# Two edge chunks to a PSUM bank: TensorE up to 12 chunks ahead of VectorE, one semaphore step a pair

## What is computed

```python
h = jnp.maximum(_layernorm(x, axis=-1), 0.0)
hx = jnp.einsum('ni,rio->rno', h, weight)          # 8 relations
msg = hx[edge_type, src]
agg = jax.ops.segment_sum(msg, dst, num_segments=num_nodes)
out = x + agg * 0.5 ** 0.5 + h_bias + (h @ loop_weight) * 0.5 ** 0.5
```

## Time and profile before

| what | value |
|---|---|
| median of the runs | 2552.59 us |
| lowest and highest run | 2542.56 and 2552.97 us |
| span of the profiled execution | 2587.3 us |
| busy: PE, POOL, DVE, ACT | 1645.8, 1552.6, 1297.6, 345.3 us |
| chunks, gathers by GpSimd, tiles | 1661, 1542, 98 |

### The profile page before, as it was taken

How to read it: one execution, slowest core, us unless ns; L and a number is a source line. 1 busy time by engine, 2 the same in 40 slices (tenths; PEclk the granted TensorE clock), 3 DMA queues, 4 the chain that set the end, 5 groups by cost and what they waited for, 6 DMA issues and landing times.

```text
span 2587.3 us, 36344 instructions
## 1 busy us (share of the span) xinstructions
PE 1645.8 (64%) x10568; PEld 1254.5 (48%) x10568; DVE 1297.6 (50%) x4142; ACT 345.3 (13%) x427; POOL 1552.6 (60%) x1646
## 2 busy tenths in 40 slices
PE   0002657766776777777777577667667777767767
PEld 0001445555554555555555455555455555545556
DVE  3273454455454555555455455455544554545444
ACT  2163010110111011011011011111111110111110
POOL 7704666666665666666666666666665666666663
PEclk9999778787877887787887787787787787777779
DMA  6554333333333333333333333333333333333332
GB/s 232 178 194 150 95 107 98 109 108 99 108 108 101 105 107 107 102 108 105 105 105 105 98 106 105 107 105 104 106 101 105 106 105 105 106 99 107 106 107 70
DMA packets 133929, 290.10 MB, mean 112 GB/s; under 512 B 34511, under 2 KB 77387, under 8 KB 130655
## 3 DMA queue, kind: packets, MB, share of 16 engines
q0 software_dynamic: 78624, 214.80, 29.0%
q10 hardware_dynamic: 49922, 54.25, 6.5%
q1 hardware_dynamic: 5180, 18.71, 2.2%
HBM read 262.02 MB, written 25.60 MB: 111 GB/s over the span
## 4 chain that ended last, share of the span: by engine, by line
PE 50%; DVE 18%; another core or an unknown queue 15%; issue 12%; DMA 2%; DVEq 1%; ACT 0%; POOL 0%; POOLq 0%; SPq 0%; ACTq 0%
PE psum L958 32%; PE psum L1022 15%; DVE room L825 10%; DVE onehot L751 3%; DMA h_table<-room 2%; PE psum L963 2%; PE psum L1008 1%; DVE stats L614 1%; DVE result L776 1%; DVEq L813 1%; DVE raw_onehot L748 1%; DMA room<-x 1%; DVEq L825 0%; ACT psum L476 0%
## 5 line engine op out<-in xcount | busy, mean ns | idle before, releaser
L410 POOL DMA_INDIRECT rows<-h_table,src_i x1542 | 1459.5, 946 | 978.3 <-issue 483.2
L825 DVE TENSOR_TENSOR room<-room,psum 128x256 f32 x1661 | 694.6, 418 | 1085.2 <-remote 502.1
L958 PE MATMUL psum<-w_sb,room 128*128 128x256 f32 x3104 | 1081.9, 469 | 161.8 <-DVE result L776 87.9
L1022 PE MATMUL psum<-onehot,rows 128*128 128x128 f16 x6260 | 711.1, 241 | 543.2 <-issue 329.5
L1022 PEld LDWEIGHTS psum<-onehot,rows 128*128 128x128 f16 x6260 | 515.9, 108 | 837.6 <-issue 449.2
L958 PEld LDWEIGHTS psum<-w_sb,room 128*128 128x128 f32 x3104 | 632.0, 231 | 245.6 <-issue 110.3
L751 DVE TENSOR_SCALAR onehot<-lane,base_i 128x128 f16<-128x128 f16 x1565 | 437.2, 280 | 66.4 <-DVE room L825 1.6
L499 ACT COPY room<-zeros 128x2048 f32<-128x2048 f32 x94 | 178.4, 1898 | 1874.7 <-DVE result L779 1099.2
L963 PE MATMUL psum<-w_sb,own_hT 128*128 128x256 f32 x384 | 129.6, 420 | 9.4 <-issue 9.3
L1063 PE MATMUL psum<-unfit_p,ones 128*1 128x6 f32 x2 | 0.2, 170 | 201.6 <-DVE room L656 201.6
L399 POOL DMA_INDIRECT raw<-x,src_i x96 | 92.1, 959 | 31.1 <-issue 28.9
(11 more groups left out here) (68 smaller groups left out, 254.4 us busy)
## 6 DMA issues: line engine op xcount, KB each, us to landing
rows<-h_table ACTq DMA_DIRECT2D x2944, 1.0 KB
rows<-h_table,src_i POOLq DMA_INDIRECT x1542
own<-h_table ACTq DMA_DIRECT2D x97, 128.0 KB
own_x<-x ACTq DMA_DIRECT2D x97, 128.0 KB
out<-result ACTq DMA_DIRECT2D x97, 128.0 KB
room<-x SPq DMA_DIRECT2D x12, 1024.0 KB
h_table<-room ACTq DMA_DIRECT2D x12, 1024.0 KB
w_sb<-weight SPq DMA_DIRECT2D x2, 1024.0 KB
```

The source lines that it names most:

```text
L410: nc.gpsimd.indirect_dma_start(out=rows[:, q % NB, :], out_offset=None, in_=table[:, :], in_offset=bass.IndirectOffsetOnAxis(ap=src_i[:, c ...
L825: nc.vector.tensor_tensor(window, window, sum_of(c).rearrange("p (a w) -> p a w", w=W), ALU.add).then_inc(added, 1)
L958: nc.tensor.matmul(ps_out[:, 0:D], nodes[:, m, :], w_sb[:, h, r, :], start=(m == 0), stop=False)
L1022: last = nc.tensor.matmul(sum_of(c)[:, h * P:(h + 1) * P], now[:, part * D + h * P:part * D + (h + 1) * P], onehot[:, k, :], start=(part = ...
```

## The change

Two chunks now share a PSUM bank: chunk c takes half c mod 2 of bank (c // 2) mod 6. A bank goes from TensorE to VectorE and back as a whole. There are still two adds of VectorE for a pair, in the same form. TensorE raises the semaphore once a pair, behind its second chunk. Where chunk c was waited for, it is now the pair that holds it (`pairs_with`): by VectorE ahead of the first add of a pair, by GpSimd ahead of every fourth gather, by ScalarE ahead of its row fetches. TensorE waits for room once a pair too: the fourth matmul of an odd chunk c waits until chunk c - 10 has been added.

```diff
-        NSUM = 6
+        BANKS = 6
+        NSUM = 2 * BANKS
...
-        last_out = sums[E_CHUNKS % NSUM]
+        PAIRS = -(-E_CHUNKS // 2)
+        last_out = sums[PAIRS % BANKS]
...
-            return sums[c % NSUM][:, 0:HR * W]
+            return sums[c // 2 % BANKS][:, c % 2 * HR * W:(c % 2 + 1) * HR * W]
+
+        def pairs_with(c):
+            return c // 2 + 1
+
+        def ends_pair(c):
+            return c % 2 == 1 or c == E_CHUNKS - 1
...
                 if q >= NB and (q - NB) % NB_STEP == 0:
-                    pool.wait_ge(summed, gathered[q - NB + NB_STEP - 1] + 1)
+                    pool.wait_ge(summed, pairs_with(gathered[q - NB + NB_STEP - 1]))
...
-                    act.wait_ge(summed, scalar_chunks[j - AB] + 1)
+                    act.wait_ge(summed, pairs_with(scalar_chunks[j - AB]))
...
-                    dve.wait_ge(summed, c + 1)
+                    if c % 2 == 0:
+                        dve.wait_ge(summed, pairs_with(c))
...
-                pe.wait_ge(added, E_CHUNKS - NSUM + 1)
+                pe.wait_ge(added, 2 * (PAIRS - BANKS + 1))
...
-                if i == 3 and NSUM <= after < E_CHUNKS:
-                    pe.wait_ge(added, after - NSUM + 1)
+                if i == 3 and NSUM <= after < E_CHUNKS and after % 2 == 0:
+                    pe.wait_ge(added, after - NSUM + 2)
...
-                    last.then_inc(summed, 1)
+                    if ends_pair(c):
+                        last.then_inc(summed, 1)
```

More of the change, by code:

```diff
@@ L160, in relational_graph_layer @@
         zeros_row = room[:, 0:HR * P]
-        NSUM = 6
+        BANKS = 6
+        NSUM = 2 * BANKS
         psum = pb("psum", [P, 8, 512], fp32)
-        sums = [psum[:, i, :] for i in range(NSUM)]
+        sums = [psum[:, i, :] for i in range(BANKS)]
         ps_out = psum[:, 6, :]
@@ L223, in relational_graph_layer @@
         onehot_ready = sem("onehot_ready")
-        summed = sem("chunk_summed")
+        summed = sem("pair_summed")
         added = sem("chunk_added")
```

## The result

The changed kernel took 2602.97 us, median of 4 runs (2582.96 to 2605.28), the kernel before on the same chip 2552.78 us (4 runs, 2542.56 to 2559.06): a ratio of 1.0183, 95% interval 1.0143 to 1.0224. The change costs 1.8%; 2.8% less was forecast. The profiled execution has a span of 2601.7 us. That of before had 2587.3 us, itself 34.7 us above its median, so the 14 us between the spans tell less than the runs do: 36 of the 50 us between the medians stand in no trace.

A forecast was written before the change was run, and what follows sets the result against it. It took TensorE's late-arriving semaphore steps, with GpSimd's resulting pauses, as the bound. Terms -88 + 20 - 4 = -72 us took the 2587.3 us span to 2515, scaled by 0.9866 to 2482 us (-2.8%); range 2378 to 2575 us.

The forecast's parts named there:

- What bounds the kernel: TensorE's sums are ready but its semaphore steps arrive late, held by back-to-back gathers; GpSimd's pauses, 416 us, largely its own doing.
- Its split of the pauses: GpSimd's pauses: 100 ended by "remote" wait for held steps (177 us); the other 144 begin or end beside TensorE's real work.
- Room for 12: TensorE's waits for room at the sums vanish, but the stall moves to the first product's wait for scaling: nothing.
- One step a pair: A held TensorE step tells of two chunks, so more GpSimd waits find what they need: -88 us, half of 177.
- Rounding up to pairs: Half of GpSimd's 381 waits ask for one chunk more, up to 1.14 us later inside the products: +20 us.
- starts the first of a pair later by as much, but catches up at 0.67 us a chunk: VectorE's adds: the delay to a pair's first chunk is made up in later adds; no cost in the sum.
- The start: GpSimd's 4.11 us pause for the eighth chunk, at 243.88, goes because four pair steps would do: -4 us.
- The shared bank: VectorE's adds keep their form and the bank is handed over whole, so no row was expected to grow.
- an estimate of 22 us less: 830 fewer TensorE semaphore increments at 26.3 ns each; left out of the sum because the trace shows no such tail.
- rival 3: Pairs ask too much in GpSimd's wait inside the products: slower, 2630 us in full, 2590 at half; chance 0.13.
- Rival 4: TensorE's idle time becomes one long wait before the products, which start at a lower clock: 2580 us; chance 0.06.
- Rival 1: The wait just moves to the `product_scaled` gate and pairs bring nothing: 2549 to 2568 us in runs; chance 0.17.

The follow-up runs named there:

- e5: The kernel before, unchanged, run again for its profile on a chip without late semaphore steps: 2081.64 us, ratio 0.9998, profiled span 2079.8 us.
- e13: Kernel before with one semaphore step a pair, banks and room for 6 sums as before, on a late chip: 2622.9 us, ratio 1.0186.
- e9: The kernel before on all eight cores at once, loops for other inputs left out: profiled medians 2631.8 us on die 0, 2081.7 us on die 1.
- e10: The changed kernel on all eight cores at once, loops for other inputs left out: profiled medians 2724.3 us on die 0, 2085.9 us on die 1.
- e14: The changed kernel with pairs counted from each step's first chunk, k = 16 alone, on a late chip: 2568.07 us, ratio 1.0063.
- e16: The changed kernel with a semaphore step after every chunk, VectorE still waiting for both chunks of a pair, on a late chip: 2598.08 us, ratio 1.0084.
- e1: Kernel before with one semaphore step a pair, banks and room as before, on a prompt chip: 2083.14 us, ratio 1.0018.

## Why the prediction was wrong

**What bounds the kernel.** Right in the main for late chips: TensorE's steps come late, and GpSimd's pauses are most of the difference to a prompt one. The pauses of before are 497.6 us in 252 waits; less the 0.30 us that stand between any two gathers, they are 422 of the 507.5 us between the spans of before and e5 (2587.3 and 2079.8 us). Another 83 us are the longer first part, which the prediction didn't look at. Its split of the pauses was off: it took the 100 "remote" ones for those that wait for a held step and the other 144 for TensorE's real work. In the trace of before the chunk that was asked for had been summed when the last gather ended in 196 of the 252.

**Room for 12, costed at nothing.** Right beside pair steps, and shown twice: by the waits of TensorE, which moved to the product, and by e13, which loses the same without the room.

**One step a pair, -88 us. This is the step that failed.** It assumed that a step which gets through singly would tell of two chunks, so that "More of GpSimd's waits find what they need". The start of the main part shows what became of that (VectorE's adds of chunks 4 and 6, then GpSimd, after):

```profile
223.91 0.42 DVE L834 TENSOR_TENSOR room<-room,psum 128x256 f32 x1 [5.08 <-PE psum L1031]
236.53 0.42 DVE L834 TENSOR_TENSOR room<-room,psum 128x256 f32 x1 [10.63 <-remote]
```
```profile
236.67 0.94 POOL L418 DMA_INDIRECT rows<-h_table,src_i  x1 [3.90 <-remote]
```

Before, single steps came 4.9 to 7.7 us apart; these two pair steps are 12.6 us apart. Each tells of two chunks, yet the eighth chunk is added 32 us after the first gather, as before, and GpSimd's pause stays. In the main part the single ones did get through and told of two (99 of 106 times VectorE then made just two adds). But there were fewer of them: where no step had come for over 2.5 us and the next came beside a running gather, it came alone; this happened 155 times before and 110 times after (e13: 116). Half as many steps are raised, and fewer pass in this way; they brought 155 chunks before and about 220 after, not 310. (The trace holds 1513 of the 1661 updates before and 787 of 831 after, so these counts are rough.) I sorted GpSimd's pauses by whether the chunk or pair asked for had been summed when the last gather ended. Of these held pauses there were 196 (383.0 us) before and 188 (350.5 us) after: 32 us saved, not 88. "remote" didn't halve. In the profiles of e9 and e10 nothing at all was saved: the four late cores together have 1616 us of held pauses before and 1642 us after.

**Rounding up to pairs, +20 us.** Undersized. The pauses in which TensorE was truly not done went from 56 (114.6 us) to 66 (168.2 us), +54 us, and on the late cores of e9 and e10 by 73 to 89 us each. e13 has 97 (235.5 us); there held pauses did fall to 156 (301.2 us), close to the gain that was forecast, and the true pauses took back more than that. e14 has 68 (131.6 us) and e16 60 (123.9 us). As these fall with the straddling undone as well as with exact steps, they aren't all GpSimd's own rounding. I take it that products which start late make the chunks among them late; no run shows this by itself. Between the profiles of before and after the pauses so grew by 54 - 32 = 21 us, and the first part was 7 us shorter (first gather at 212.57 and 205.53 us), which gives their 14 us. The medians of the runs differ by 50 us. Where the other 36 arise isn't seen, since the profiled execution of before was 34.7 us above its median.

**VectorE "starts the first of a pair later by as much, but catches up at 0.67 us a chunk".** This was the other half of the error: a cost left at nothing. It catches up in adds, but the scaling stands behind k = 1 in its list, and in every second step both k = 16 ahead of it and k = 1 open a pair. TensorE had finished k = 2 within 0.2 to 1.5 us behind k = 1, so by the matmuls it costs nearly nothing; but what VectorE waits for is k = 2's step, which held it up by 3.13 us in the turn above. Undoing both straddling pairs (e14) is worth 1.2%, some 30 us. The pairs (k = 16, 0) and (1, 2) of every second step stand in the section on the change, ahead of the prediction, which gave them no term.

**The start, -4 us,** didn't come: the same gather waits 3.90 us at 236.67, shown above, against 4.11 us. **The shared bank** did as forecast (adds 417 ns). The rule of the Trainium skill, "TensorE: Matmul & The Clock Gate", section "The cost: per-tile semaphore tail", that each serialised increment costs 26.3 ns (it is given there for matmuls packed as tiles into the array), made for an estimate of 22 us less. No run shows this gain: on a prompt chip e1, with 830 fewer steps, came 3.8 us above before (2083.14 to 2079.32), though GpSimd is the bound there and could hide it.

**The rivals.** The sign is that of rival 3, pairs ask too much, given 0.13. Its price at half, 2590 us, was near; its place was not. It was put into GpSimd's wait inside the products, and two thirds of the loss hang on the pairs that straddle VectorE's way to the scaling. Of its two conditions one was met (fewer than a quarter of the held pauses went: 8 of 196), the other not (66 of 254 pauses are true ones, not over a third). Rival 4 didn't come: the clock was 0.809 over the execution, and 0.79 in the window of the earlier trace rows, where before had 0.80. Rival 1's reading of the pair step, that it brings little, was nearer than mine; its price of 20 us for rounding was as much too small. The range ended at 2575 us and left more above it than the stated 0.1: rivals 3 and 4 had 0.19 together.

## What to carry over

Before a semaphore is made coarser, look at each waiter for the place where it needs the first of the group and something else stands behind it; count the groups so that they don't straddle that place or the way to it (1.2% of 1.8% here). When the trace shows signals that arrive long after they were raised, don't take it that fewer of them arrive just as often: measure how many come singly. And a delay of a signal may come from outside of the kernel, so compare with the kernel before on the same chip at the same time, and know of which kind the measurement is before an experiment is read.

## What the runs showed of the hardware

I hadn't expected that the late steps depend on where and when a kernel is run, down to the die. The same kernel took 2550 to 2581 us on late chips and 2079 to 2085 us on prompt ones, some 470 to 500 us or 23%; in one run of eight cores die 0 took 2558.6 to 2712.0 us and die 1 2053.4 to 2110.0 us. On late chips, after 2.5 us without a step, one of TensorE's semaphore that comes beside running gathers of GpSimd's comes alone (mean burst 1.0 updates), and one in a pause in bursts (3.3 before, with steps a chunk). Steps of VectorE come late too, in the first part (waits of ScalarE for them of up to 28.5 us, ended by "remote"). TensorE's mean granted clock was 0.81 in late profiles and mostly 0.89 in prompt ones. A lower clock doesn't make a core late: in e10's profiled execution die 1 had 0.826 and took 2085.9 us. Why one die is late and another not, and whether a chip stays so, is not shown by any run.
